# Rings of four for the expert slots' rows, metas, results and indices, and mixed weights loaded two pieces a slot

## The reference

```python
def _combine_weights(xt, gate_w):          # top 2 of 4 groups, then top K=4 of E=16 experts
    ...
out = jnp.zeros_like(xt)
for e in range(E):
    a = _swiglu(xt @ expert_up_w[e].T)     # 512 -> 2*352, silu(gate) * up
    out = out + cw[:, e:e + 1] * (a @ expert_down_w[e].T)
out = out + _swiglu(xt @ shared_up_w.T) @ shared_down_w.T
...
x = x + _L0_ffn_ref(_layernorm(x), ...)
```

## Time and profile before

| | us |
|---|---|
| median of 3 runs | 1296.19 (1291.11 to 1301.31) |
| profiled execution, its time | 1297.71 |
| its span in the trace | 1295.9 |
| PE busy | 1232.2 (95%) |
| DVE busy | 844.3 (65%) |
| ACT busy | 366.9 (28%) |
| POOL busy | 340.1 (26%) |

### The profile page before, as it was taken

How to read it: one execution, slowest core, us unless ns; L and a number is a source line. 1 busy time by engine, 2 the same in 40 slices (tenths; PEclk the granted TensorE clock), 3 DMA queues, 4 the chain that set the end, 5 groups by cost and what they waited for, 6 DMA issues and landing times.

```text
span 1295.9 us, 26339 instructions
## 1 busy us (share of the span) xinstructions
PE 1232.2 (95%) x8747; PEld 747.5 (58%) x8747; DVE 844.3 (65%) x2352; ACT 366.9 (28%) x808; POOL 340.1 (26%) x401
## 2 busy tenths in 40 slices
PE   7979999999998999999999999999999899999995
PEld 6857777877776555444444555554555455554552
DVE  4897688768769475244511577676767676876772
ACT  4754656654453323220000011111111111111111
POOL 1202324322333122114653012121212222121212
PEclk9989999998998999999999999999999999999998
DMA  5443953753663595275446876959596877868562
GB/s 165 83 60 85 146 122 79 155 129 66 129 128 125 131 218 116 89 242 190 174 179 235 254 198 159 221 115 233 125 254 153 227 179 194 197 177 216 124 151 25
DMA packets 205089, 202.41 MB, mean 156 GB/s; under 512 B 71584, under 2 KB 153504, under 8 KB 202912
## 3 DMA queue, kind: packets, MB, share of 16 engines
q1 hardware_dynamic: 120864, 112.25, 32.9%
q10 hardware_dynamic: 67456, 54.24, 16.8%
q0 software_dynamic: 16640, 34.24, 12.6%
HBM read 123.76 MB, written 81.08 MB: 158 GB/s over the span
## 4 chain that ended last, share of the span: by engine, by line
PE 46%; DMA 7%; ACTq 2%; issue 1%; DVE 1%; ACT 0%; POOLq 0%; DVEq 0%
PE pD L2423 10%; PE pG L2410 10%; PE pU L2410 9%; DMA xs<-slot_rows 5%; PE pD L2391 4%; PE pG L2372 4%; PE pU L2372 4%; PE pD L2420 2%; PE pG L2406 2%; PE pU L2406 1%; DMA out<-y,ix_mixed 1%; ACTq L2209 1%; ACTq L2223 1%; PE pU L2366 1%; PE pD L2386 0%
## 5 line engine op out<-in xcount | busy, mean ns | idle before, releaser
L2299 DVE STREAM_TRANSPOSE ups<-a 32x96 f32<-32x96 f32 (+1 forms) x1136 | 296.6, 261 | 35.2
L2183 POOL DMA_INDIRECT out<-y,ix x64 | 99.7, 1558 | 392.9 <-DVE ix L2323 178.5
L2410 PE MATMUL pG<-w,xsT 128*128 x512 | 167.4, 470 | 15.2 <-DVE xsT L2288 13.7
L2423 PE MATMUL pD<-w,ups 128*128 (+1 forms) x384 | 178.2, 599 | 1.9 <-DVE ups L2299 0.7
L2410 PE MATMUL pU<-w,xsT 128*128 x512 | 162.0, 459 | 0.0
L973 PE MATMUL pProj<-front_region 128*128 128x256 f32 x624 | 155.6, 393 | 2.2 <-ACT front_region L708 1.6
L2410 PEld LDWEIGHTS pG<-w,xsT 128*128 128x128 f32 x512 | 96.7, 192 | 94.9 <-issue 54.6
L2239 ACT ACTIVATE g<-pG 128x352 f32<-128x352 f32 x72 | 33.4, 464 | 367.0 <-DVE ix L2323 173.6
L2410 PEld LDWEIGHTS pU<-w,xsT 128*128 128x128 f32 x512 | 97.5, 190 | 54.5 <-issue 0.5
L973 PEld LDWEIGHTS pProj<-front_region 128*128 128x128 f32 x624 | 113.8, 192 | 20.4 <-ACT front_region L708 2.1
L2423 PEld LDWEIGHTS pD<-w,ups 128*128 128x128 f32 (+1 forms) x384 | 70.7, 190 | 85.8 <-issue 78.7
(11 more groups left out here) (312 smaller groups left out, 1787.1 us busy)
## 6 DMA issues: line engine op xcount, KB each, us to landing
w<-in_expert_T SPq DMA_DIRECT2D x16, 1920.0 KB, 8.8
front_region<-in_expert_T ACTq DMA_DIRECT2D x64, 352.0 KB
slot_rows<-zeros SPq DMA_DIRECT2D x72, 266.0 KB, 7.3
xs<-slot_rows ACTq DMA_DIRECT2D x288, 64.0 KB
front_region<-in_expert_T ACTq DMA_DIRECT2D x32, 256.0 KB
front_region<-in_L_attn_hidden_states SPq DMA_DIRECT2D x16, 256.0 KB, 4.2
x2r<-in_L_attn_hidden_states SPq DMA_DIRECT2D x16, 256.0 KB, 4.8
partial_sums<-x2r SPq DMA_DIRECT2D x16, 256.0 KB, 3.2
```

The costliest lines, as they stand in the source:

```text
L2183: pool.indirect_dma_start(out=flat, out_offset=bass.IndirectOffsetOnAxis(ap=to[:, 0:1], axis=0), in_=y[1 - par][:, :], in_offset=None, bou ...
L2299: dve.transpose(aT[par][B * to:B * to + B, 0:n, rows], a[rows, 0:len(IC) * P].rearrange("p (c n) -> p c n", c=len(IC))[:, 0:n, B * to:B * ...
L2410: mm = pe.matmul(out[:, 0:I], rows[:, k, :], w[:, bass.ds(weights[0], 1), 2 * I * k + at:2 * I * k + at + I], start=(k == 0), stop=(k == D ...
L2423: return pe.matmul(out[:, :], gated_[0:m, c, :], w[0:m, bass.ds(weights[0], 1), at:at + D], start=(c == 0), stop=(c == 2))
```

## The change

Four things are changed.

The buffers of rows (xs), metas (mt), results (y) and indices (wq, ix) become rings of RING=4. xs and y now lie in xg, the two input buffers of the shared expert, in front_region; so in the trace of the changed kernel these tiles are called front_region. The guards reach four slots back in place of two.

The rows of slot q+4 are asked for in body(q), at the place where those of q+2 were; at the start two slots' rows are asked for in body(1) and body(2). The meta of slot q+2 is asked for in body(q), where that of q+1 was.

PIECES is 2, so the 14 pieces take seven slots, not five. They begin in the body after the mixed slot before (part_of), where they began two bodies after it.

The mixed slots are q = 7, 16, 25, 34, 43, 52, 60 and 68. The "until" list is adapted: its value is at most one slot later than before.

```diff
-STEP = NQ // NM
-MIXED = STEP - 2
+MIXED_AT = [9 * m + 7 - max(0, m - NM + 3) for m in range(NM)]
-PIECES = 3
+PIECES = 2
+RING, AHEAD = 4, 2
...
-            link(dve.tensor_copy(done_i[:, :], lm[:, :]))
+            link(dve.tensor_scalar(done_i[:, :], lm[:, :], 2.0, None, ALU.add))
...
-    xs = [sb(f"xs{i}", [P, D]) for i in range(2)]
+    xs = [xg[0][:, i, :] for i in range(RING)]
-    y = [sb(f"y{i}", [P, D]) for i in range(2)]
-    mt = [sb(f"mt{i}", [P, RW - D]) for i in range(2)]
+    y = [xg[1][:, i, :] for i in range(RING)]
+    mt = [sb(f"mt{i}", [P, RW - D]) for i in range(RING)]
...
+            def load_rows(q):
+
+                least(act, s_xT, q - RING + 1)
+                for b in range(BLOCKS):
+                    act.dma_start(xs[q % RING][B * b:B * b + B, :].rearrange("p (a c) -> p a c", a=BLOCKS),
+                                  xv[block_of(q)][:, :, P * b:P * b + P]).then_inc(s_xl[q % RING], 16)
+
+            def load_meta(q):
+
+                least(act, s_ex, q - RING + 1)
+                act.dma_start(mt[q % RING][:, :], mv[block_of(q)][:, D:RW]).then_inc(s_ml[q % RING], 16)
+
+            def rows_by(q):
+
+                return min(NQ, q + 1 + AHEAD + min(q, RING - AHEAD))
+
+            def part_of(q):
+
+                for m in range(NM):
+                    begin = MIXED_AT[m - 1] + 1 if m else 0
+                    if begin <= q < begin + DC + len(IC):
+                        return m, q - begin
+                return None
...
-                    load_rows(0, 0)
-                    load_meta(0, 0)
-                    load_rows(1, 1)
-                if q < NQ - 2:
-                    load_rows(q + 2, par)
-                if not last(q):
-                    load_meta(q + 1, 1 - par)
+                    load_rows(0)
+                    load_meta(0)
+                    load_rows(1)
+                    load_meta(1)
+                for r in range(max(2, rows_by(q - 1)), rows_by(q)):
+                    load_rows(r)
+                if q + AHEAD < NQ:
+                    load_meta(q + AHEAD)
...
-                    least(act, s_add, 16 * adds_before(q - 2))
+                    least(act, s_add, 16 * adds_before(q - RING))
...
-                if PIECES * (q % STEP) < 2 * (DC + len(IC)) and q < NQ:
-                    load_mixed(q // STEP, q % STEP)
+                if part_of(q):
+                    load_mixed(*part_of(q))
...
-                least(dve, s_y, q - 1)
-                least(dve, s_add, 16 * adds_before(q - 1))
+                least(dve, s_y, q - RING + 1)
+                least(dve, s_add, 16 * adds_before(q - RING + 1))
...
-                        pe.wait_ge(s_wm, 32 * (DC + len(IC)) * (q // STEP + 1))
+                        pe.wait_ge(s_wm, 32 * (DC + len(IC)) * (before_mixed(q) + 1))
```

More of the change, by code:

```diff
@@ L1782 @@
 NQ = NF + NM
-STEP = NQ // NM
-MIXED = STEP - 2
+MIXED_AT = [9 * m + 7 - max(0, m - NM + 3) for m in range(NM)]
 NS = 3
-PIECES = 3
+PIECES = 2
+RING, AHEAD = 4, 2
 def is_mixed(q):
-    return q % STEP == MIXED
+    return q in MIXED_AT
 def before_mixed(q):
-    return max(0, (q + STEP - 1 - MIXED) // STEP)
+    return sum(at < q for at in MIXED_AT)
 def adds_before(q):
@@ L1804, in block_of @@
 def block_of(q):
-    return NF + q // STEP if is_mixed(q) else q - before_mixed(q)
+    return NF + before_mixed(q) if is_mixed(q) else q - before_mixed(q)
 assert sorted(block_of(q) for q in range(NQ)) == list(range(NQ))
-assert all(q == i + (i + 1) // 8 for q in range(NQ) if not is_mixed(q) for i in [block_of(q)])
+assert all(q <= i + (i + 3) // 8 <= q + 1 for q in range(NQ) if not is_mixed(q) for i in [block_of(q)])
 def routing(nc, es, counts, scratch, lg, xall, pos, lists, s_pos, s_read, s_routed, route, s_xall):
@@ L2039, in experts @@
     eye = sb("eye", [P, P])
-    y = [sb(f"y{i}", [P, D]) for i in range(2)]
-    mt = [sb(f"mt{i}", [P, RW - D]) for i in range(2)]
-    wq, ix = [sb(f"wq{i}", [P, 1]) for i in range(2)], [sb(f"ix{i}", [P, 1], I32) for i in range(2)]
+    y = [xg[1][:, i, :] for i in range(RING)]
+    mt = [sb(f"mt{i}", [P, RW - D]) for i in range(RING)]
+    wq, ix = [sb(f"wq{i}", [P, 1]) for i in range(RING)], [sb(f"ix{i}", [P, 1], I32) for i in range(RING)]
     ixm = [sb(f"ix_mixed{i}", [P, 1], I32) for i in range(2)]
@@ L2057, in experts @@
     s_scat = [sem(f"rows_scattered{i}") for i in range(2)]
-    s_xl, s_ml = [sem(f"slots_loaded{i}") for i in range(2)], [sem(f"slot_meta{i}") for i in range(2)]
+    s_xl, s_ml = [sem(f"slots_loaded{i}") for i in range(RING)], [sem(f"slot_meta{i}") for i in range(RING)]
     s_add, s_ex, s_base = sem("rows_added"), sem("meta_taken"), sem("base_stored")
@@ L2180, in body @@
                 for h in range(2 if is_mixed(q - 1) else 1):
-                    to = ixm[h] if is_mixed(q - 1) else ix[1 - par]
+                    to = ixm[h] if is_mixed(q - 1) else ix[(q - 1) % RING]
                     least(pool, s_add, 16 * (adds_before(q - 1) + h))
                     pool.indirect_dma_start(out=flat, out_offset=bass.IndirectOffsetOnAxis(ap=to[:, 0:1], axis=0),
-                                            in_=y[1 - par][:, :], in_offset=None, bounds_check=T - 1, oob_is_err=False,
+                                            in_=y[(q - 1) % RING][:, :], in_offset=None, bounds_check=T - 1, oob_is_err=False,
                                             compute_op=ALU.add).then_inc(s_add, 16)
@@ L2247, in body @@
                     act.wait_ge(s_ex, q)
-                    least(act, s_add, 16 * adds_before(q - 2))
-                    act.activation(y[1 - par][:, :], (pYlast if end(q) else pYq)[:, :], ACT.Copy, scale=wq[1 - par][:, 0:1]).then_inc(s_y, 1)
+                    least(act, s_add, 16 * adds_before(q - RING))
+                    act.activation(y[(q - 1) % RING][:, :], (pYlast if end(q) else pYq)[:, :], ACT.Copy,
+                                   scale=wq[(q - 1) % RING][:, 0:1]).then_inc(s_y, 1)
                 if first(q):
                     act.wait_ge(s_routed, 1)
-                if PIECES * (q % STEP) < 2 * (DC + len(IC)) and q < NQ:
-                    load_mixed(q // STEP, q % STEP)
+                if part_of(q):
+                    load_mixed(*part_of(q))
             route_act(act)
@@ L2284, in turn_rows @@
             def turn_rows(q, par):
-                dve.wait_ge(s_xl[par], (q - par) * 32 + 64)
+                dve.wait_ge(s_xl[q % RING], 64 * (q // RING + 1))
                 least(dve, s_up, q - 1)
                 dve.transpose(xsT[par][:, :, :].rearrange("p k (a i) -> p a k i", a=BLOCKS),
-                              xs[par][:, :].rearrange("p (a k j) -> p a k j", a=BLOCKS, k=DC)).then_inc(s_xT, 1)
+                              xs[q % RING][:, :].rearrange("p (a k j) -> p a k j", a=BLOCKS, k=DC)).then_inc(s_xT, 1)
             def turn_gated(q, par):
@@ L2301, in turn_gated, with take_meta @@
                            .then_inc(s_aT, 1)
-            def take_meta(q, par):
+            def take_meta(q):
+                r = q % RING
                 if is_mixed(q):
                     of_half = [dve.value_load(lists["mixed"][0:1, i:i + 1], min_val=0, max_val=E - 1)
-                               for i in (2 * (q // STEP), 2 * (q // STEP) + 1)]
+                               for i in (2 * before_mixed(q), 2 * before_mixed(q) + 1)]
                 else:
@@ L2310, in take_meta @@
                     expert = dve.value_load(lists["expert"][0:1, i:i + 1], min_val=0, max_val=E - 1)
-                dve.wait_ge(s_ml[par], (q - par) * 8 + 16)
-                least(dve, s_y, q - 1)
-                least(dve, s_add, 16 * adds_before(q - 1))
+                dve.wait_ge(s_ml[r], 16 * (q // RING + 1))
+                least(dve, s_y, q - RING + 1)
+                least(dve, s_add, 16 * adds_before(q - RING + 1))
                 if is_mixed(q):
@@ L2317, in take_meta @@
                         rows = slice(HR * h, HR * h + HR)
-                        dve.tensor_copy(wq[par][rows, :], mt[par][rows, bass.ds(of_half[h], 1)])
-                        ins = dve.tensor_scalar(ixm[h][rows, :], mt[par][rows, E:E + 1], -1.0, float(T), ALU.mult, ALU.add)
+                        dve.tensor_copy(wq[r][rows, :], mt[r][rows, bass.ds(of_half[h], 1)])
+                        ins = dve.tensor_scalar(ixm[h][rows, :], mt[r][rows, E:E + 1], -1.0, float(T), ALU.mult, ALU.add)
                     ins.then_inc(s_ex, 1)
                 else:
-                    dve.tensor_copy(wq[par][:, :], mt[par][:, bass.ds(expert, 1)])
-                    dve.tensor_scalar(ix[par][:, :], mt[par][:, E:E + 1], -1.0, float(T), ALU.mult, ALU.add).then_inc(s_ex, 1)
+                    dve.tensor_copy(wq[r][:, :], mt[r][:, bass.ds(expert, 1)])
+                    dve.tensor_scalar(ix[r][:, :], mt[r][:, E:E + 1], -1.0, float(T), ALU.mult, ALU.add).then_inc(s_ex, 1)
             def body(q, par):
@@ L2338, in body @@
                         turn_gated(q, par)
```

(2 more changed lines are left out.)

7 lines of the change are left out of this document (removed).

## The result

The changed kernel took 1322.44 us (median of 4 runs, 1319.88 to 1325.41), against 1293.65 for the kernel before in the same rounds: a ratio of 1.022, interval 1.0186 to 1.0255. It is 28.8 us slower. The forecast was 1292, with a range of 1278 to 1304.

What follows compares the result with a forecast made beforehand. PE was taken to bound the kernel, slowed by late rows; -21 (rings) - 3.6 (end) + 20.6 (new stalls) = -4.0 us takes 1297.7 to 1293.7, and the median, 1.5 lower, to 1292; range 1278 to 1304.

Steps and rivals of the forecast that it cites:

- What bounds the kernel: Whole kernel: PE, busy for 1232.2 of 1295.9 us, loses about 3 us a cycle in six cycles, mostly to late rows.
- Part 1, the gain: Full slots: rings and rows asked for earlier end PE's waits for transposed rows and silus, a gain of 21 us.
- The room of the adds: Scatter-adds on POOL: 51.4 us of adds in a cycle of 66 to 71, so a ring absorbs a late one.
- rival C: Full slots: adds outlast a slot, the ring ends and half the gain stays out, 10.5 us more, 1303; chance 0.1.
- Part 2, the new wait: Gates of slots 7, 60 and 68: PE waits about 5.5 us each for last pieces; 20.6 us with restarts and clock.
- Here the queues are quiet: Last pieces of slots 7, 60 and 68: no expert load beside them, so a piece lands in 3.2 us.
- the wait of nothing: Mixed slots 16, 25, 34, 43 and 52: last pieces go out a whole slot early, so no wait was counted.
- rival B: Mixed slots: last pieces land in 10.5 us, three stalls of 12.8, other five begin to wait; about 1316, chance 0.12.
- The clock: Gates behind the new stalls: PE's clock falls in two of three, 1.67 us each, 3.3 us in all.
- Part 3, the end: End of the kernel: moving the mixed slot from 70 to 68 takes one add away, 3.6 us less.
- nothing takes its place: End of the kernel: the last y is ready before slot 70's add lands, so the removed add's 3.58 us are won.
- The Trainium skill's price: Landing of a 192 KB piece: about 2.0 us plus bytes at 436 GB/s, 2.45 us; each stall would be 4.7.

Runs made afterwards that it cites:

- e7: e6 with rows asked for two slots ahead, as in the kernel before, rings and looser guards kept: 1292.95 us, ratio 0.9979.
- e8: e6 with the last mixed slots back at 61 and 70, so the kernel before with only rings and earlier rows: 1279.46 us, ratio 0.9877.
- e1: The changed kernel with three mixed pieces a slot again, all else kept: 1298.07 us, ratio 1.0015.
- e6: e1 with the mixed pieces begun two bodies after the mixed slot, as in the kernel before: 1281.31 us, ratio 0.9891.
- e5: e1 without the second scatter-add of each mixed slot: 1277.01 us, ratio 0.9857.
- e10: The changed kernel with the down pieces on their own semaphore, so a mixed slot's gate waits only for up pieces: 1293.23 us, ratio 0.9994.

## Why the prediction was wrong

**What bounds the kernel**: right in what it saw, and short of one bound. PE's waits in the full slots came from late rows (e7). The chain of adds stood beside it unseen. Before, the adds ran from 735.70 to 1287.42, and in these 551.7 us the chain was idle for only 20 beyond its hand-overs.

**Part 1, the gain**: the mechanism was right (e7), and the size near in the changed kernel, 25 us against 21. But that held only while PE's new stalls gave the adds time. With three pieces, where nothing else is changed (e8), the rings gave 15.

**The room of the adds** in part 1: wrong. "8 x 5.5 + 2 x 3.7 = 51.4 us in a cycle of 66 to 71" took the median landing. It left out that the next add is issued only some 0.8 us after a landing and that landings in full traffic are far above the median (up to 11.1 us before, 12.1 after; the mean of the full ones before is 6.4). With means and hand-overs it is 8 x 7.2 + 2 x 4.5, about 67 us, as long as the fastest cycle. In e1 the ten adds from one mixed slot to the next went from 791.21 to 860.30, 69.1 us, which is more than a cycle of PE without stalls (67.5). This is rival C's mechanism. It cost no wait in the changed kernel itself, where PE's stalls gave the adds time, and 17 to 21 us in e1, by e6 and e5.

**Part 2, the new wait**: the mechanism was right where it was looked for, its size wrong, and this decided: 20.6 us were forecast and 56.2 measured. The step that failed is the sentence "Here the queues are quiet: the expert loads of SP fall in other slots". With it failed the wait of nothing given to slots 16, 25, 34 and 52, because their last pieces go out "one whole slot ahead of need". SP's loads fall on the last pieces of five of eight mixed slots. I had the rows of one such load at hand only as a price, and didn't lay the issue times of SP beside the slots' starts with the right count: SP waits for the down matmuls of a slot, and these come at the end of the next body. Without such a load the estimate held for the whole, less so for its terms: slots 7 and 68 waited 5.48 and 4.35 us against 5.5 forecast. From the end of PE's last matmul to the second issue it was 2.4 and 1.8 us (forecast 1.9), to the landing 3.0 and 2.5 (3.2), and to PE's start 0.1 (0.35). The other five, which the forecast took to wait not at all (16, 25, 34, 52) or 5.5 (60), waited 30.4 us in place of 5.5. This is rival B, at 1316 us the nearest of all cases, to which I gave 0.12. Its number is in part luck. Of the three stalls that it put at 12.8 us only one, of 13.34, was so long. The other five, which it said "begin to wait too" and priced at nothing, were 17.5 of the 40.6 us.

**The clock**: forecast to fall in two of three stalls, it fell in all seven over 1 us. Each cost 1.3 to 2.4 us in its gate and not 1.67, so 13.9, with the up matmuls 15.6, in place of 3.3.

**Part 3, the end**: right in kind, too large. From the start of slot 71's gate to the end of the span it is 23.3 us (1300.33 to 1323.6) against 25.3 (1270.61 to 1295.9), 2 us in place of 3.6; from the end of the last matmul, which the forecast meant, 12.9 against 14.3, only 1.4. The add that takes the place of two mixed ones is longer: 5.68 us from its issue to the next one, against 3.46:

```profile
1309.64 1.55 POOL L2183 DMA_INDIRECT out<-front_region,ix  x1 [4.93 <-ACT front_region L2262]
1315.32 1.56 POOL L2183 DMA_INDIRECT out<-front_region,ix  x1 [4.13 <-DMA out<-front_region,ix]
```

Even this gain needs the stalls. In e1, e6 and e10, which have the new places and no wait ahead of slots 60 and 68, the end took 28.0, 29.7 and 28.9 us, more than the 25.3 before, since the chain of adds was behind. So "nothing takes its place" failed too.

**The Trainium skill's price** (DMA: Bandwidth & Descriptors, Anatomy of one DMA), an estimate of 2.45 us for 192 KB: the trace after agrees where no expert's load is on the way, with 2.7 us ahead of slot 7 and 2.4 ahead of slot 68. That estimate does not give the 9.2 to 9.7 beside an expert's load, and that was the price that mattered.

## What to carry to other kernels

When a load is spread thinner, write down for each use how far ahead its last piece is asked for, and which other queue's bursts fall on that moment; a quiet price holds only if both are checked, by the same count of slots on each engine. A serial chain, such as adds that wait for each other, has to be measured from start to start over its whole length, since a median landing hides the hand-over and the slow tail; here it was nearly as long as the matmuls. Look at its idle time as well, since its mean interval follows the length of the run. Of a bundle of edits, try the one that removes the wait alone: rings with earlier rows gave 1.2%, and with the rest of the bundle it became 2.2% slower.

## What the runs showed of the hardware

A transfer of 192 KB landed in 2.4 to 3.0 us with no expert's load on the way. It took 7.0 to 10.7 us when SP asked for 1920 KB within 2 us of it, though ACT asks on a queue of its own. An indirect add of 128 rows took 5.7 us from issue to the next issue in the quiet end, and one of which only the 64 rows of one half are in bounds 3.5. From an add's landing to the next add's start were some 0.8 us. TensorE's granted clock was 0.50 to 0.66 over the gates behind every one of the seven stalls of 3.9 to 13.3 us, that is 1.2 of 2.4 GHz for all or a part of them. In the kernel before it was 0.60 behind two of the six stalls of 1.75 to 2.8 us, and 1.00 behind the other four.
